# A 7x7 deformed convolution on normalised images: new start of the program, accumulator seeds issued in a row, shifted copies in two parts per unit

## What is computed

```python
x: (32, 32, 56, 56) float32;  weight (32, 32, 9);  P (2, 32, 9);  bias (32,)
g = (x - mean(x, (2, 3))) / sqrt(var(x, (2, 3)) + 1e-5)
kern = zeros(32, 32, 7, 7)            # from weight and P, four bilinear corners for each point
out = x + conv(g, kern, padding=3) + bias
```

## Time and profile before

| | us |
|---|---|
| median of 3 runs | 328.8 |
| the runs | 326.24, 328.80, 332.79 |
| the profiled execution, its own time | 326.01 |
| its span in the trace | 324.2 |

### The profile page before, as it was taken

One profiled execution on the slowest core, in us unless ns is written; L12 is line 12 of the kernel. 1 busy time (PEld: TensorE's weight loads), 2 busy tenths in 40 slices (PEclk: granted clock), 3 DMA queues, 4 the chain that ended last, 5 costly groups with the idle time before them and its releaser, 6 DMA issues.

```text
span 324.2 us, 9588 instructions
## 1 busy us (share of the span) xinstructions
PE 289.6 (89%) x3380; PEld 201.7 (62%) x3380; DVE 273.1 (84%) x454; ACT 218.6 (67%) x327; POOL 155.0 (48%) x259
## 2 busy tenths in 40 slices
PE   5920589999999989999999989999999999999990
PEld 2700466666666657776677766677877666766760
DVE  4489598999898888989899989989998989897331
ACT  2369796967868676967696788778796868461300
POOL 6232545645363727374564527372929274644000
PEclk9975599999999999999999999999999999999997
DMA  8953354989898896979797989999898939489605
GB/s 141 151 110 85 88 140 96 255 196 242 186 217 215 195 236 146 265 167 255 156 259 173 237 189 193 254 189 255 168 260 176 262 78 243 107 223 235 135 12 99
DMA packets 128253, 59.07 MB, mean 182 GB/s; under 512 B 122068, under 2 KB 122068, under 8 KB 128228
## 3 DMA queue, kind: packets, MB, share of 16 engines
q1 hardware_dynamic: 115204, 24.90, 40.9%
q0 software_dynamic: 9312, 33.04, 36.8%
q10 hardware_dynamic: 3712, 0.80, 1.4%
HBM read 12.88 MB, written 12.85 MB: 79 GB/s over the span
## 4 chain that ended last, share of the span: by engine, by line
PE 57%; DVE 9%; SPq 9%; issue 8%; DMA 7%; POOL 3%; ACT 3%; DVEq 0%; ACTq 0%; POOLq 0%
PE ps_s L802 17%; PE ps_x L802 16%; PE ps_y L802 12%; PE ps_eo L802 8%; SPq L196 6%; DMA xraw<-x 4%; DVE e L451 3%; SPq L186 3%; DVE d L451 2%; DMA xb<-xs 2%; DVE xs L472 2%; POOL xn L702 2%; PE ps_eo L770 1%; POOL xb L690 1%; DMA wnat<-L_conv_weight 1%
## 5 line engine op out<-in xcount | busy, mean ns | idle before, releaser
L690 POOL DMA_DIRECT2D xb<-xs x192 | 93.5, 494 | 62.0 <-DVE xs L472 59.3
L802 PE MATMUL ps_s<-xb,w 128*64 128x392 f16 (+1 forms) x576 | 103.4, 329 | 0.9 <-DMA xb<-xs 0.8
L802 PE MATMUL ps_s<-xs,w 128*64 128x392 f16 (+1 forms) x576 | 103.9, 329 | 0.2 <-ACT m L349 0.2
L702 POOL TENSOR_SCALAR xn<-xraw,scale,offset 32x784 f32<-32x784 f32 x32 | 55.0, 1724 | 79.3 <-DVE offset L448 79.3
L802 PEld LDWEIGHTS ps_s<-xs,w 128*64 128x64 f16 x576 | 62.4, 110 | 22.0 <-issue 1.5
L802 PEld LDWEIGHTS ps_s<-xb,w 128*64 128x64 f16 x576 | 62.3, 110 | 9.2 <-DMA xb<-xs 2.2
L802 PE MATMUL ps_x<-xs,w 128*64 128x392 f16 x384 | 66.5, 329 | 0.1
L802 PE MATMUL ps_x<-xb,w 128*64 128x392 f16 x384 | 66.6, 329 | 0.0
L343 ACT ACTIVATE xs<-e 128x900 f16<-128x900 f32 x48 | 59.1, 1230 | 10.3 <-DVE e L451 6.4
L802 PE MATMUL ps_eo<-xb,w 128*64 128x392 f16 (+1 forms) x384 | 65.5, 326 | 0.0
L802 PE MATMUL ps_eo<-xs,w 128*64 128x392 f16 (+1 forms) x384 | 65.5, 326 | 0.0
(11 more groups left out here) (90 smaller groups left out, 403.7 us busy)
## 6 DMA issues: line engine op xcount, KB each, us to landing
xb<-xs POOLq DMA_DIRECT2D x96, 168.8 KB, 4.1
xb<-xs POOLq DMA_DIRECT2D x96, 166.9 KB, 4.4
xraw<-x SPq DMA_DIRECT2D x124, 98.0 KB, 2.9
out<-result SPq DMA_DIRECT2D x124, 98.0 KB, 5.0
xraw<-x ACTq DMA_DIRECT2D x4, 98.0 KB, 3.9
out<-result ACTq DMA_DIRECT2D x4, 98.0 KB, 3.7
wnat<-L_conv_weight POOLq DMA_DIRECT2D x1, 36.0 KB, 3.8
pts<-L_conv_P POOLq DMA_DIRECT2D x2, 1.1 KB, 3.1
```

The source lines that it names most:

```text
L690: pool.dma_start(dst[32 * g:32 * g + 32, 0:run - line * past], src[32 * f:32 * f + 32, line * past:run]).then_inc(shifted[par][b], DMA)
L702: pool.tensor_scalar(xn[96:128, u % 2, :, SLOTS * m:SLOTS * m + ROWS, 1:1 + SIDE // 2], image(u % RING, m)[96:128, :].rearrange("p (n w k) ...
L802: last = pe.matmul(into[p:p + HALF, :, 0:PER * wide], w[:, n // 2, s, q, t, :], moving.rearrange("p n q m -> p n (q m)"), start=fresh and ...
```

## The change

1. **Start.** P and weight are loaded by SP instead of POOL. SP issues three and ACT five of the first unit's eight loads, the first image has its own semaphore, and unit 1's load waits until unit 0 has landed. POOL issues unit 2's load. The fold matrix is made without the 7 selections. The statistics of unit 0 are folded between the blocks of the filter product, image by image. One image of the last group is normalised by VectorE, and half of the filter scaling is done by ACT. PE has 12 idle matmuls in place of 8 at the start and up to 20 more before the first stream.
2. **Unit 0 by pieces.** Its shifted copies of streams 0; 1, 2; 3; 4, 5 (PIECES) are issued half by SP and half by POOL, each piece as soon as it is ready; the differences and filter parts are interleaved with them, and DVE does outs_0, outs_1 and outs_2 of unit 0 between the batches of units 0 and 1.
3. **Folds of units 2 and 3.** PE folds unit 2 at stream 2 of unit 1 (before: at stream 4 of unit 0), and unit 3 at stream 7 of unit 1 (before: at stream 4 of unit 1). From unit 2 on nothing changes there.
4. **Seeds.** In each step both seeds are issued directly behind `middle` on ACT, where the second stood behind the sums and four `high`.
5. **Shifted copies.** From unit 1 on there are two parts, streams 0 to 2 and streams 3 to 8, so 8 DMAs a unit. The part of six streams is issued when all nine streams are ready, and PE waits for the whole of it at s = 3.
6. **Last store.** The store of the last unit's first image waits only for that image's last output step.

```diff
+PIECES = [(0, 1), (1, 2), (3, 1), (4, 2)]
+PARTS = [(0, 3), (3, 6)]
...
 # gpsimd
-            normalise(0)
-            for u in range(UNITS):
-                shift(u, u % 2, 0)
-                if u == 0:
-                    shift(u, u % 2, 1)
+            normalise(0, (0,))
+            for n, (s, count) in enumerate(PIECES):
+                pool.wait_ge(hi_ready, s + count)
+                pool.wait_ge(lo_ready, s + count)
+                shift(pool, 0, s, count, (1, 3), piece_shifted_too[n])
+            shift_part(0, 0, 1, 6, 3)
+            normalise(1)
+            for u in range(1, UNITS):
+                shift_part(u, u % 2, 0, *PARTS[0])
                 if u + 1 < UNITS:
                     normalise(u + 1)
-                if u:
-                    shift(u, u % 2, 1)
-                shift(u, u % 2, 2)
+                shift_part(u, u % 2, 1, *PARTS[1])
...
 # tensor
-            for u in range(2):
-                step(u, u, 0, True, True, first=u == 0)
...
+            for s in range(NS):
+                if s == 0:
+                    pe.wait_ge(combined, 5)
+                if s == 2:
+                    both_moments(2)
+                if s == 3:
+                    pe.wait_ge(m11_ready, 2)
+                if s == 4:
+                    pe.wait_ge(seeded, 3)
+                if s == 6:
+                    pe.wait_ge(combined, OUTS + 2)
+                if s == 7:
+                    both_moments(3)
+                    pe.wait_ge(seeded, 4)
+                convolve(1, 1, s, 0)
...
 # scalar, step
-                middle(u, first)
-                seed(u, h, 0, first)
+                middle(u)
+                for k in range(2):
+                    seed(u, h, k)
                 if early:
                     sums(u + 3, (h + 3) % RING, nth)
...
-                seed(u, h, 1, first)
...
 # vector, unit 0 (the tail of its order)
+            outs_1(0)
             spread(1)
             rstd(1)
+            outs_2(0, 0, 0)
+            odd_differences(1, 1)
             mean(2)
...
+            low(1, 1, *BATCHES[1])
+            outs_3(0)
+            second_differences(1, 0)
+            second_differences(1, 2)
+            outs_4(0, 0)
+            low(1, 1, *BATCHES[2])
+            low(1, 1, *BATCHES[3])
+            spread(2)
+            rstd(2)
+            mean(3)
+            low(1, 1, *BATCHES[4])
+            low(1, 1, *BATCHES[5])
+            dve.wait_ge(lo_ready, 2 * NS)
+            step(1, 1, 0, True, True, True)
```

More of the change, by code:

```diff
@@ L271, in store @@
                         put(sp, u, par, m, g)
-            load(0, 0, (0, 1))
+            sp.dma_start(pts[:, :, :], P.rearrange("t c (a k) -> (c a) t k", a=CHUNKS)).then_inc(points_loaded, DMA)
+            sp.dma_start(wnat[:, :], weight.rearrange("o c k -> o (c k)")).then_inc(weights_loaded, DMA)
+            fetch(sp, 0, 0, 0, 0)
+            fetch(sp, 0, 0, 0, 1)
+            fetch(sp, 0, 0, 1, 0)
+            sp.wait_ge(image_loaded, LOAD // PER)
+            sp.wait_ge(x_loaded[0], loaded(0, 0))
             load(1, 1)
@@ L293, in _ @@
         def _(act):
-            for m in range(PER):
-                for g in (2, 3):
-                    fetch(act, 0, 0, m, g)
+            fetch(act, 0, 0, 0, 2)
+            fetch(act, 0, 0, 0, 3)
+            for g in (1, 2, 3):
+                fetch(act, 0, 0, 1, g)
             act.wait_ge(ones_built, 1)
@@ L360, in seed, with step @@
                                ACT.Copy, scale=scales[:, 2:3]).then_inc(seeded, 1)
-            def step(u, h, nth, nxt, stats, early, first=False, second=False):
+            def step(u, h, nth, nxt, stats, early):
                 a = 1 - h % 2
                 if nxt:
-                    high(u + 1, a, *BATCHES[0], first=first)
+                    high(u + 1, a, *BATCHES[0])
                 if stats:
@@ L375, in step @@
                     for batch in BATCHES[2:]:
-                        high(u + 1, a, *batch, first=first)
-                seed(u, h, 1, first)
+                        high(u + 1, a, *batch)
                 if stats:
@@ L646, in _ @@
         def _(pool):
-            for t in range(2):
-                pool.dma_start(pts[:, t, :], P[t:t + 1].rearrange("t c (a k) -> (t c a) k", a=CHUNKS)
-                               ).then_inc(points_loaded, DMA)
-            pool.dma_start(wnat[:, :], weight.rearrange("o c k -> o (c k)")).then_inc(weights_loaded, DMA)
             pool.memset(ident[:, :], 0.0).then_inc(ident_built, 1)
@@ L714, in _, with warm @@
+            normalise(1)
+            for u in range(1, UNITS):
+                shift_part(u, u % 2, 0, *PARTS[0])
                 if u + 1 < UNITS:
                     normalise(u + 1)
-                if u:
-                    shift(u, u % 2, 1)
-                shift(u, u % 2, 2)
+                shift_part(u, u % 2, 1, *PARTS[1])
         @block.tensor
         def _(pe):
+            def warm(count):
+                for n in range(count):
+                    last = pe.matmul(ps_y[:, n % 2, 0:N], zeros[:, 0:128], zeros[:, 0:N], start=True, stop=True)
+                return last
@@ L723, in _ @@
             pe.wait_ge(zeros_built, 1)
-            for n in range(8):
-                last = pe.matmul(ps_y[:, n % 2, 0:N], zeros[:, 0:128], zeros[:, 0:N], start=True, stop=True)
-            last.then_inc(marked, 1)
+            warm(12)
             pe.wait_ge(weights_loaded, DMA)
@@ L733, in _, with fold_columns @@
             pe.wait_ge(wmax_ready, 1)
-            pe.matmul(ps_stat[0:1, 8:8 + CH], wmax[:, :], ident[:, :], start=True, stop=True).then_inc(wmax_row, 1)
-            def fold_columns(a, b):
+            pe.matmul(ps_y[0:1, 1, 0:CH], wmax[:, :], ident[:, :], start=True, stop=True).then_inc(wmax_row, 1)
+            def fold_columns(into, a, b):
                 for p in (0, HALF):
-                    last = pe.matmul(ps_stat[p:p + HALF, a:b], fold[:, p:p + HALF], moments[:, a:b],
+                    last = pe.matmul(into[p:p + HALF, :], fold[:, p:p + HALF], moments[:, a:b],
                                      start=True, stop=True)
-                last.then_inc(folded, 1)
+                return last
             def mean(u):
@@ L774, in _ @@
                         last.then_inc(kern_in_psum, 1)
-            pe.wait_ge(srow_step, 7)
-            pe.matmul(ps_s[:, 128:131], ones[:, :], srow[:, 2:5], start=True, stop=True).then_inc(scales_in_psum, 1)
-            variance(0)
             pe.wait_ge(kern_ready, 2)
@@ L793, in convolve @@
                 fresh = s not in (4, 5, 7, 8)
+                piece = [p for p, _ in PIECES].index(s) if nth is None and s in (0, 1, 3, 4) else None
                 for c, (n, q, t) in enumerate(order):
@@ L806, in convolve, with step @@
                 last.then_inc(conv_done, 1)
-            def step(u, par, nth, stats, early, first=False):
+            def step(u, par, nth, stats, early):
                 for s in range(NS):
-                    if s == 0 and not first:
+                    if s == 0:
                         pe.wait_ge(combined, OUTS * (u - 1) + 5)
```

287 lines of the change are left out of this document (196 added, 91 removed).

## The result

The changed kernel takes 364.4 us in the median, where the kernel before takes 329.4 in the same comparison: a ratio of 1.109, with a 95% interval of 1.099 to 1.120. It is slower by 35 us. The direction was forecast. The size was not: 343 was predicted, with 352 as the upper end. Runs of most versions lie at two levels some 6 us apart, and ratios compare the lower ones.

A forecast was written before the change was run, and what follows sets the result against it. It took PE to bound the kernel, with steady units moving to a loop through VectorE, GpSimd and copies. 326.0 + 15.6 (to unit 2) + 2.1 (steady) + 0.5 (last units) - 0.5 (last store) = 343.7, given as 343; range 333 to 352.

The forecast's parts named there:

- What bounds the kernel: Whole kernel: PE busy 289.6 of 324.2 us, steady units lose 0.67 us each, little slack elsewhere.
- The start of unit 0: Unit 0: offset ready at 16.6, first difference at 19.6 instead of 22.6, first stream at about 24.7 instead of 36.1.
- VectorE spends what is won: Units 0 and 1: added VectorE work uses up the 3 us; low 1 of unit 1 ends at 46.5, before 45.1.
- Unit 1's moved folds: Unit 1: folds behind late copies on a slow clock; mark of unit 2 at 97.4 instead of 81.81, +15.6 us.
- The steady units: Units 2 to 12: a loop through VectorE, GpSimd and copies of 17.7 us against 17.49, +2 over 10 units.
- First term: Steady unit, from stream 4's start through VectorE's steps and GpSimd's last group to the copies' issue: 7.1 us.
- Second term: Steady unit, from first issue to last landing of the six-stream copies: 8.6 us, with 7.0 to 10.1 as ends.
- Third term: Steady unit, stream 3 on PE after the copies land, up to the next unit's mark: 2.0 us.
- The last three units: Units 12 to 15, without loads: copies land in about 8.1 us, +0.5 us.
- Larger DMAs land sooner: Rival on the six-stream copies: landing in 7.7 us or less, steady units 16.8, total about 333; chance 0.15.
- The seeds in a row: ScalarE's second seed moved ahead of four highs and the sums: counted as nothing, since SP is still busy with stores.
- The case of 351 and more: Rival: copies hinder each other more, landing in 9.3 to 10.1 us, loop 18.4 to 19.2; chance 0.17.

The follow-up runs named there:

- small_stores: Changed kernel with each store DMA cut to one of the 14 output rows of each channel, same DMA count: 348.8 us, 1.059 of the kernel before.
- seeds_only: Kernel before with only the second seed moved up directly behind the first: 331.2 us, against 330.9 for the kernel before.
- m_early: Changed kernel with three copy parts, earlier folds of units 2 and 3, ScalarE's m and seeds earlier in unit 1: 328.3 us, 0.992 of the kernel before.
- m_early_fill: m_early with three idle matmuls more, between the turning of the weight and the filter blocks: 329.6 us, 0.996 of the kernel before.
- low5_first: Changed kernel with VectorE's last subtraction of a unit (low of streams 7 and 8) ahead of outs_2: 362.1 us, 1.097 of the kernel before.
- warm3: Changed kernel with eight idle matmuls ahead of PE's wait for the copies at stream 3, from unit 2 on: 367.3 us, 1.116 of the kernel before.

## Why the prediction was right and wrong

- **What bounds the kernel** was right in the main. The steady units had 0.67 us above TensorE's own work, and the changed ones are bound by the loop through VectorE, GpSimd and the copies.
- **The start of unit 0** came out earlier than forecast: offset ready at 14.6 (16.6), first difference 17.4 (19.6), first stream 21.4 (24.7). The blocks began 1.9 earlier (1.6 was taken), and the first took 1.95 us where it had taken 3.5 before: there it had run at half the rate. I had counted the time between the folds of the earlier trace rows for all blocks and overlooked that the first was slower.
- **VectorE spends what is won** was right, but the step is mis-sized. From the first difference to the end of low 1 of unit 1 I had 26.9 us; it took 31.1 (17.4 to 48.5). The 4.04 of the row at 43.92 is nearly all of the difference: I didn't follow the mean of unit 2 to its place ahead of stream 7, which stands behind copies that land at 40.4. So the early 2.2 and the late 4.2 partly cancel, and that the mark of unit 2 came out only 2.5 off is in part luck.
- **Unit 1's moved folds** were right in each step, 2 to 3.5 us later throughout: unit 2's fold at 59.2 (57.1), VectorE idle before its variance for 5.52 (5 forecast), the part issued at 64.78 (62.2), unit 3's fold at 82.8 (80.4), unit 2 at 90.3 (86.8). PE's rows here:

```profile
69.12 0.54 PE L935 MATMUL ps_s<-xs,w 128*64 128x392 f16 x1 [7.60 <-ACT m L409]
...
72.89 0.54 PE L935 MATMUL ps_s<-xb,w 128*64 128x392 f16 x1 [3.23 <-DMA xb<-xs]
...
90.26 0.35 PE L935 MATMUL ps_s<-xs,w 128*64 128x392 f16 x1 [4.08 <-DVE part L563]
```

  I hadn't seen the 7.60 for m. It costs little, since the copies come 3.2 later. The clock did what was forecast: it was low after the stretches in which PE stood still. In the last of these rows PE is busy 1.65 of 8 us.

```profile
54.00:58.00 4.00, 3.89 (x32) 2.49 (x34) 0.10 (x1) 0.00 (x0) 0.00 (x0) 0.65 0.58 118
...
66.00:74.00 8.00, 1.65 (x9) 0.80 (x11) 7.43 (x8) 8.00 (x14) 2.70 (x6) 0.50 0.98 231
```

- **The steady units are the step that failed.** The sum was 7.1 + 8.6 + 2.0 = 17.7, and the trace has 19.28: 0.85 of the difference in the first term, 0.35 in the second, 0.38 in the third. Ten units make 16 of the 20 us that are missing. *First term:* I let outs_1 follow the mark at once and let VectorE's work run without gaps. VectorE arrives later, and GpSimd's last group begins 4.05 behind the mark. Then come 3.12 for the group and 0.78 of waiting for the low of streams 7 and 8, which stands behind outs_2. The kernel before would have told me: there the issue comes 8.5 behind the mark in the mean of ten units, and in unit 1, whose rows I had the earlier trace rows, 8.3. One such unit, from its mark to the issue:

```profile
135.21 0.33 PE L802 MATMUL ps_x<-xs,w 128*64 128x392 f16 x1
...
140.00 3.59 POOL L702 TENSOR_SCALAR xn<-xraw,scale,offset 32x784 f32<-32x784 f32 x2 [4.23 <-DVE offset L448]
143.54 3.91 POOL L690 DMA_DIRECT2D xb<-xs  x8
```

  It didn't matter there, because TensorE had slack behind the issue. With 8.5 the sum would have been 19.1, or +16 where I had +2. *Second term:* I took the middle of the range, and the mean of 8.95 lies a little above it. It alternates between 8.0 to 8.2 and 9.1 to 10.0; small_stores shows the stores to be most of the reason. *Third term:* it is 1.95 in five units and 2.4 to 3.2 in the others, in two of them because the clock fell in the wait and in three because the fold waited for ScalarE's sums. I had given neither a price here. The last three units are mis-sized too: my own terms make 7.1 + 8.1 + 2.0 = 17.2 against 16.8, which is 1.1 and not 0.5, and it was 1.9.
- **"Larger DMAs land sooner"** fell. A 337.5 KB copy takes 5.6 us in the median and a 168.8 KB one 3.7; the signs that I named were 6 to 7 for this forecast and 5.5 for its failure. The median was near the second, and the time near neither: PE waits for the last of four, and that one took 7.9 in the slow unit. A median of landings was the wrong sign to name. The Trainium skill's rule of batching to 1 MiB or more ("DMA: Bandwidth & Descriptors", Measured) is stated for one DMA from HBM to SBUF. The copies here go within SBUF and grew from 169 to 337 KB, so its figure was no price for them, and no run here tests the rule at its own size. For this step the measurement decides: 1.095 for the two parts alone.
- **The seeds in a row** at nothing: right for the kernel before (seeds_only), open for two parts. **The fewer issues on GpSimd** at nothing: right.
- **The range** was too narrow on the slow side. The case of 351 and more had a chance of 0.17 and a price from rows, and by its own terms it ran from 351 to 359; the range cut it off at 352. The sum itself was 343.7, which rounds to 344 and not to 343.

## What to carry to other kernels

A loop through several engines has to be measured from mark to mark in the trace of before, also where it isn't the bound: its slack hides that the parts are longer than their instructions. Before transfers are put together, ask who waits for the first byte and who for the last; a consumer that could start on a third of the data pays for all of it, and in this kernel it paid the most in the units where loads and stores came at the same time. And where a statistic's tiny matmul stands behind a stream that waits for data, the next unit can wait with it: here this cost 11.9 us.

## What was unexpected in the hardware

- **Two speeds at one granted clock.** The start has two forms. The same four block matmuls, in the changed kernel and in m_early:

```profile
6.85 1.10 PE L897 MATMUL ps_eo<-cols,diag 96*128 96x256 f32 x4 [0.46 <-DVE cols L660]
```

```profile
7.00 2.05 PE L907 MATMUL ps_eo<-cols,diag 96*128 96x256 f32 x4 [0.41 <-DVE cols L666]
```

  The profile gives a granted clock of 1.00 for both. The kernel before shows both speeds in one execution, also at 1.00: its first blocks take 2.05 and 1.91, a later one 1.03.

```profile
8.74 2.05 PE L770 MATMUL ps_eo<-cols,diag 96*128 96x256 f32 x4 [1.11 <-DVE cols L574]
...
13.54 1.03 PE L770 MATMUL ps_x<-cols,diag 96*128 96x256 f32 x4
```

  In m_early all blocks up to 18 run at the longer time, and the first stream comes at 27.8 instead of 21.4. Such a start stood in the profiles of four of the eleven versions with the new prologue, and most of it reaches the mark of unit 2 (106.5 and 105.1 against 99.9). It doesn't alone decide how long an execution takes: m_early_fill's profiled one had the early start and took 330.4. The Trainium skill ("TensorE: Matmul & The Clock Gate", Part 1) says that the number of slow matmuls at a kernel's start varies from run to run, and that the recorded clock events aren't always reliable; the traces agree with both, with starts 6.4 us apart and 1.00 recorded at either speed. That it is the clock is likely and not shown.
- **VectorE and GpSimd stretch each other.** The last group takes 2.65 and the subtraction 1.92 in one unit, 3.60 and 1.19 in the next. The Trainium skill ("SBUF — State Buffer", Who interferes with whom) says that a VectorE instruction with two inputs from SBUF contends with a GpSimd instruction that reads SBUF. The trace agrees: the stretched subtraction ends 1.07 us behind the end of the group (185.12 and 184.05), about its usual length, as if it had begun there, and in low5_first no subtraction is stretched and every group takes 3.6.
- **Idle matmuls aren't free, even in a wait.** In warm3 they kept the clock at 1.00 where it had been 0.54 and gave back 0.38 of the 1.80 us, and they cost 0.95 a unit where PE hardly waits.
- What stays open: how much of the late landing is due to the loads. small_stores kept them, and 8.0 us from issue to landing were left. Open too is what the seeds in a row are worth with two parts.
